# Hybrid transformer block: first stage unrolled into slots over a ring of three PSUM banks, exponentials scaled on GpSimd

## The reference

```python
x = x + _L0_attn_a_ref(_layernorm(x, axis=-1), L0_attn_a_Wq, ..., L0_attn_a_Wpost)
...
Q, K, V = X @ Wq, X @ Wk, X @ Wv          # 16 heads of 64
raw_attn = jnp.einsum('bshe,bthe->bsth', Q, K * inv_sqrt_d)
attn = jax.nn.softmax(raw_attn, axis=2)
A = jnp.einsum('bsth,bthe->bshe', attn, V)
A = jax.nn.gelu(A, approximate=False)
P = A @ Wpost
return X + P
```

## Time and profile before

| | |
|---|---|
| Median of 3 runs | 4349.55 us (4342.45 to 4356.19) |
| Profiled execution | 4354.61 us, span 4352.8 us, mean granted TensorE clock 0.963 |
| PE busy | 3920.6 us (90%) |
| DVE busy | 2631.3 us (60%) |
| ACT busy | 2414.3 us (55%) |
| POOL busy | 800.1 us (18%) |
| First stage | from the start to about 2449 us of the span |

### The profile page before, as it was taken

The page is one execution under the profiler, slowest core; times in us unless marked ns, Lnnn a source line. Parts: engine busy times, 40 slices in busy tenths (PEclk is TensorE's granted clock), DMA queues, the critical chain, the costliest instruction groups (busy, mean ns, idle before and its releaser), DMA issues. The chain is left out here.

```text
span 4352.8 us, 65779 instructions
## 1 busy us (share of the span) xinstructions
PE 3920.6 (90%) x24194; PEld 2770.9 (64%) x24194; DVE 2631.3 (60%) x3989; ACT 2414.3 (55%) x4705; POOL 800.1 (18%) x587
## 2 busy tenths in 40 slices
PE   6999999999999999999999568999999998999987
PEld 5777777777777777777777444555555555555544
DVE  5666666566656656665666446666666666666552
ACT  3565556556555655555565325555555555555554
POOL 0000000000000000000000143444444444343422
PEclk9999999999999999999999779999999999999998
DMA  4344334434333443443344222222222222222220
GB/s 120 81 106 97 83 88 97 98 78 107 88 85 85 92 99 84 100 97 83 79 106 93 62 49 45 50 50 50 50 50 50 50 50 50 49 49 48 45 43 15
DMA packets 152325, 315.67 MB, mean 73 GB/s; under 512 B 23072, under 2 KB 76704, under 8 KB 152032
## 3 DMA queue, kind: packets, MB, share of 16 engines
q1 hardware_dynamic: 152032, 311.39, 33.8%
HBM read 33.43 MB, written 25.17 MB: 13 GB/s over the span
## 5 line engine op out<-in xcount | busy, mean ns | idle before, releaser
L586 DVE TENSOR_REDUCE neg_max<-ps_s 128x2 f32<-128x1024 f32 x512 | 624.8, 1221 | 487.2 <-PE ps_s L361 487.2
L1168 DVE TENSOR_REDUCE max_b<-ps_s 128x2 f32<-128x1024 f32 x512 | 624.6, 1220 | 331.6 <-PE ps_s L952 330.4
L489 ACT ACTIVATE e_a<-ps_s,neg_max 128x512 f32<-128x512 f32 x1024 | 692.4, 685 | 87.8 <-DVE neg_max L586 82.1
L1051 ACT ACTIVATE et<-ps_s 128x1024 f32<-128x1024 f32 x512 | 522.4, 1020 | 353.7 <-PE ps_s L966 351.7
L525 ACT ACTIVATE et_a<-ps_t 128x512 f32<-128x512 f32 x512 | 306.6, 599 | 545.5 <-PE ps_t L242 545.4
L360 PE MATMUL ps_s<-stack_a 128*128 128x512 f32 x1024 | 445.1, 435 | 106.3 <-issue 72.4
L242 PE MATMUL ps_t<-ident,e_a 128*128 128x128 f32 x4096 | 531.5, 273 | 4.6 <-issue 2.6
L242 PEld LDWEIGHTS ps_t<-ident,e_a 128*128 128x128 f32 x4096 | 477.1, 140 | 78.3 <-ACT et_a L525 11.5
L376 PE MATMUL ps_o<-et_a,v_a 128*64 128x256 f32 x4096 | 498.3, 385 | 0.0
L910 POOL TENSOR_TENSOR h_lo<-h,h_hi 128x512 fp32r<-128x512 f32 x256 | 325.4, 1288 | 486.2 <-ACT h_hi L1087 484.1
L361 PE MATMUL ps_s<-stack_a 128*128 128x512 f32 x1024 | 414.6, 405 | 0.0
(11 more groups left out here) (189 smaller groups left out, 7186.2 us busy)
## 6 DMA issues: line engine op xcount, KB each, us to landing
stack_a<-raw_a SPq DMA_DIRECT2D x256, 384.0 KB, 4.7
stack_a<-raw_a SPq DMA_DIRECT2D x256, 256.0 KB, 4.3
stack_a<-raw_a SPq DMA_DIRECT2D x256, 128.0 KB, 4.0
q_stack<-roped_q SPq DMA_DIRECT2D x256, 64.0 KB
k_stack<-roped_k SPq DMA_DIRECT2D x256, 64.0 KB
x_next<-X SPq DMA_DIRECT2D x16, 512.0 KB, 6.7
X<-res SPq DMA_DIRECT2D x16, 512.0 KB, 2.9
x_ahead<-X SPq DMA_DIRECT2D x16, 512.0 KB, 3.9
```

The lines of the kernel that those rows point to most:

```text
L489: ins = nc.scalar.activation(e_a[u % 2][:, j, :], ps_s[:, 2 * (u % 2) + j, :], ACT.Exp, bias=neg_max[:, u % 4, j:j + 1], accum_out=sums[:, ...
L586: nc.vector.reduce_max(neg_max[:, u % 4, :], ps_s[:, 2 * (u % 2):2 * (u % 2) + 2, :], AX.X, negate=True)\
L1051: nc.scalar.activation(et[:, v % 5, :, :], ps_s[:, 2:4, :], ACT.Exp)\
L1168: nc.vector.reduce_max(max_b[:, u // 4 % 2, :, u % 4], ps_s[:, 0:2, :], AX.X, negate=True)\
```

## The change

All units of all sequences, 512 of them, become one row of *slots* without blocks, barriers or a hardware loop. In slot `s`, PE makes the scores of unit `s + 2`, the transposes of unit `s`, in every fourth slot the values of a whole pair (32 matmuls), and then what `todo_of` lists for the slot: a transpose of x, a q or k projection, two values projections, or a quarter of the output projection. The slots count from the start of a sequence: q and k of a pair are made in slots with remainder 1 and 2 when divided by 4, the values projections and the output projection in those with remainder 3, and `values` in those with remainder 0.

Every product that leaves through a bank, the two halves of the transposes among them, takes the next bank of a ring of three (`ps_t` 0, `ps_t` 1, `ps_m`) in the order of the program, and waits until the product three places earlier has been emptied. `e_a` has three buffers in place of two, `et_a` five in place of four, `parts` five in place of four.

The softmax division moves ahead of the transposes: DVE inverts the two sums of a unit, and GpSimd multiplies the unit's exponentials (128x1024) by them in one operation, whose second operand repeats one number 512 times. `recip_rows`, the copy to `rs_a`, the spreading copy and `norm` are gone. Gelu reads `ps_o` directly, pair by pair, and GpSimd makes the low half of its split. The row sums of the output projection no longer stay in four banks for all pairs: two groups of four pairs are added to `res` one after the other.

```diff
-        def attention_a(seq, before, now, ahead):
...
+                def normalise_exps(u):
+                    pool.wait_ge(recip_ready, u + 1)
+                    factor = recip[:, u % 4, :].rearrange("p (j o) -> p j o", o=1).to_broadcast([P, 2, S])
+                    nc.gpsimd.tensor_tensor(e_a[:, u % 3, :, :], e_a[:, u % 3, :, :], factor, ALU.mult).then_inc(e_normed, 1)
+
+                def heads_low(n):
+                    pool.wait_ge(heads_high, n + 1)
+                    nc.gpsimd.tensor_tensor(parts_of(n)[:, 1, :], heads_a[:, n % 2, :], parts_of(n)[:, 0, :], ALU.subtract)\
+                        .then_inc(parts_ready, 1)
...
+                def transposes(u):
+                    pe.wait_ge(e_normed, u + 1)
+                    for part in range(2):
+                        fill = fill_of["turn", part, u]
+                        if fill >= 3:
+                            wait_emptied(pe, fill - 3)
...
+                for slot in range(FIRST, LAST):
+                    if 0 <= slot + 2 < UNITS_ALL:
+                        scores(slot + 2)
+                    if 0 <= slot < UNITS_ALL:
+                        transposes(slot)
+                    if slot % 4 == 0 and 1 <= slot // 4 <= PAIRS * BATCH:
+                        values(slot // 4 - 1)
+                    for todo in todo_of.get(slot, []):
+                        product(todo)
...
+                def gelu(n):
+                    act.wait_ge(values_done, n + 1)
+                    if n >= 2:
+                        act.wait_ge(parts_ready, n - 1)
+                    nc.scalar.activation(heads_a[:, n % 2, :], ps_o[:, :], ACT.Gelu).then_inc(gelu_done, 1)
+
+                for slot in range(FIRST, LAST):
+                    for todo in todo_of.get(slot - 1, []):
+                        high(todo)
+                    if 0 <= slot < UNITS_ALL:
+                        copy_turned(slot)
+                    if (slot - 1) % 4 == 0 and 1 <= (slot - 1) // 4 <= PAIRS * BATCH:
+                        gelu((slot - 1) // 4 - 1)
+                    if 0 <= slot + 2 < UNITS_ALL:
+                        exps(slot + 2)
...
+                for slot in range(FIRST, LAST):
+                    if 0 <= slot + 1 < UNITS_ALL:
+                        invert(slot + 1)
+                    for todo in todo_of.get(slot - 1, []):
+                        low(todo)
+                    if 0 <= slot + 2 < UNITS_ALL:
+                        unit_max(slot + 2)
+                    if 0 <= slot < UNITS_ALL:
+                        copy_turned(slot)
```

More of the change, by code:

```diff
@@ L236, in token_major, with bank, wait_filled, wait_emptied @@
             return last
[L238 to L250, removed]
+        def bank(fill):
+            return banks[fill % 3]
+        def wait_filled(engine, fill):
+            engine.wait_ge(bank_filled[fill % 3], fill // 3 + 1)
+        def wait_emptied(engine, fill):
+            engine.wait_ge(bank_freed[fill % 3], fill // 3 + 1)
+        def emptied(ins, fill):
+            ins.then_inc(bank_freed[fill % 3], 1)
         with nc.Block() as block:
@@ new lines, in hybrid_block_kernel @@
+        UNITS_ALL = BATCH * UNITS
+        XT, QK_FIRST, VALUE_SLOTS = -9, -7, ((-5, -5, -1, -1), (11, 11, 15, 15))
+        POST = ((19, 23), (35, 39))
+        STATS, AGGREGATE, POWER, NORMALISE = (-19, -18), -17, -17, (-15, -14)
+        RESIDUAL, LOAD_X, SAVE_X, STACK_FIRST = 11, -20, 40, -5
+        FIRST, LAST = -20, UNITS_ALL + 9
+        todo_of = {}
+        for s in range(BATCH):
+            for k in range(KT):
+                todo_of.setdefault(UNITS * s + XT, []).append(("x", k, 0, s))
+            for p in range(PAIRS):
+                for i in range(2):
+                    todo_of.setdefault(UNITS * s + QK_FIRST + 4 * p + i, []).append(("qk", p, i, s))
+            for g in range(2):
+                for tok in range(TB):
+                    todo_of.setdefault(UNITS * s + VALUE_SLOTS[g][tok], []).append(("v", g, tok, s))
+            for half in range(2):
+                for two in range(2):
+                    todo_of.setdefault(UNITS * s + POST[half][two], []).append(("post", half, two, s))
@@ L404, in _ @@
-                    if now:
-                        scores(0)
-                        scores(1)
-                    if before:
-                        for k in range(PAIRS):
-                            if k >= 4:
-                                pe.wait_ge(heads_split, k - 3)
-                            for t in range(TB):
-                                for i, (part, w) in enumerate(((0, wpost_hi), (0, wpost_lo), (1, wpost_hi))):
-                                    last = mm(wide_banks[t][:, 0:D], heads_parts[:, k % 4, part, t * P:(t + 1) * P],
-                                              w[:, k, :], start=(k == 0 and i == 0), stop=(k == PAIRS - 1 and i == 2))
-                                if k == PAIRS - 1:
-                                    last.then_inc(post_done, 1)
-                            if k < PAIRS - 1:
-                                last.then_inc(parts_used, 1)
@@ L457, in _ @@
-                    if ahead and not now:
-                        for k in range(KT):
-                            transpose_x(k)
-                        for m in range(3):
-                            project_ahead(m)
-                    if now:
-                        values(2 * PAIRS - 1)
-                    if ahead:
-                        project_ahead(3)
-                    if now and not ahead:
-                        pe.wait_ge(rs_ready, PAIRS - 1)
-                        recip_rows(PAIRS - 1)
@@ L469, in _ @@
-                    if ahead:
-                        for g in range(2 * TB):
-                            if g >= 4:
-                                pe.wait_ge((va_even, va_odd)[g % 2], (g - 4) // 2 + 1)
-                            token_major(ps_s[:, g % 4, :], xh_a, xl_a, wa_hi, wa_lo, g // 2, 2 * DA + (g % 2) * S, S)\
-                                .then_inc(va_proj, 1)
-                            if g == 0 and now:
-                                pe.wait_ge(lo_ready, projs + 4)
-                                recip_rows(PAIRS - 1)
@@ L680, in attention_a, with product @@
-            next_block()
-        attention_a(-1, False, False, True)
-        attention_a(0, False, True, True)
-        with nc.Fori(1, BATCH - 1) as seq:
-            attention_a(seq, True, True, True)
-        attention_a(BATCH - 1, True, True, False)
-        attention_a(BATCH, True, False, False)
+                                          et_a[:, (4 * n + 2 * half + h) % 5, t, :], start=(t == 0), stop=(t == TB - 1))
+                    last.then_inc(values_done, 1)
+                def product(todo):
+                    kind, a, b, s = todo
+                    fill = fill_of[todo]
+                    if fill >= 3:
+                        wait_emptied(pe, fill - 3)
+                    if kind == "x":
+                        pe.wait_ge(xn_ready, TB * (s + 1))
+                        for t in range(TB):
+                            last = nc.tensor.transpose(bank(fill)[:, t * P:(t + 1) * P], xn_a[:, t, a * P:(a + 1) * P], ident[:, :])
+                    elif kind == "qk":
+                        if a == 0 and b == 0:
+                            for k in range(KT):
+                                wait_emptied(pe, fill_of["x", k, 0, s])
+                        last = feature_major(bank(fill), xh_a, xl_a, wa_hi, wa_lo, b * DA + a * P)
+                    elif kind == "v":
+                        last = token_major(bank(fill), xh_a, xl_a, wa_hi, wa_lo, b, 2 * DA + a * S, S)
+                    else:
+                        pe.wait_ge(parts_ready, PAIRS * s + 4 * a + 4)
+                        for t in (2 * b, 2 * b + 1):
+                            for k in range(4):
+                                p = 4 * a + k
+                                parts = parts_of(PAIRS * s + p)
+                                for m, (part, w) in enumerate(((0, wpost_hi), (0, wpost_lo), (1, wpost_hi))):
+                                    last = mm(bank(fill)[:, (t % 2) * D:(t % 2 + 1) * D], parts[:, part, t * P:(t + 1) * P],
+                                              w[:, p, :], start=(k == 0 and m == 0), stop=(k == 3 and m == 2))
+                    last.then_inc(bank_filled[fill % 3], 1)
@@ L690, in hybrid_block_kernel @@
+        next_block()
         with nc.Block() as block:
```

528 lines of the change are left out of this document (235 added, 293 removed).

## The result

The changed kernel takes 4786.6 us (median of 4 runs, 4775.5 to 4793.7) against 4352.9 us (median of 4 runs) for the kernel before: 1.0996 times the time before, 95% interval 1.0963 to 1.1028. The profiled execution took 4787.6 us, with a span of 4785.8 us and a mean granted clock of 0.919 (before 0.963).

The account below looks back on a forecast made before the run. TensorE's own stream was taken to bound the first stage. Waits of 576 us less a gain of 310 gave +266, the clock +109: +375 on 4354.6, 4730, as median 4725 us; range 4470 to 4880.

Parts of the forecast that it names:

- the walk: Step-by-step timing of one pair through TensorE, ScalarE and VectorE in the changed order: 20.9 us, where it was 18.8.
- TensorE's own work: TensorE's matmuls for a pair in the changed order, summed from distances of starts, without waits: 16.4 us.
- gross gain: First stage: time saved if TensorE never waited, 16 sequences x 19.4 us = 310 us.
- First wait: TensorE waits before the second projection for the first projection's bank, behind Gelu and table loads: 3.75 us per pair.
- Second wait: TensorE's next product waits for the second projection's bank to be emptied: 0.75 us per pair.
- the clock: TensorE's granted clock falls after the recurring wait: 0.85 us per pair, +109 us in all.
- Half of the bound: Clock price per pair lies between 0 and 1.7 us; half of it, 0.85, was taken.
- Rival 1: The clock holds in most pairs of the first stage, so only the waits cost: 4616 us; chance 0.27.
- GpSimd: Its product with the repeated operand takes 2.40 us per unit, costs nothing, and decides only beyond 3.4 us.
- Rival 2: GpSimd becomes the bound if the repeated operand makes its product twice as dear, 4.8 us: 4950 us; chance 0.09.
- Rival 3: ScalarE's chain is shorter: 4290 us if loads cost no time, 4040 if never last; chance 0.09 together.
- Rivals 4 and 5: 4: about 2 us of chain hidden, clock holds, effects cancel, chance 0.04; 5: smaller loss, up to 4560, chance 0.08.

Follow-up runs that it names:

- e8: Changed kernel with Exp pair ahead of Gelu, both projections' high parts early, and VectorE's reciprocal behind the copy in remainder-3 slots: 4199.7 us, 0.9653 of the kernel before.
- e9: e8 with Copy in place of Gelu, so without table loads: 4174.5 us, 0.9589 of the kernel before.
- e1: Changed kernel with ScalarE's Copy in place of Gelu, so no table loads in the first stage: 4307.9 us, 0.9895 of the kernel before.
- e10: e3 with a tiny Exp right behind Gelu, so the load for Exp comes at once: 4774.2 us, 1.0968 of the kernel before.
- e2: Changed kernel with 13 idle matmuls per pair filling TensorE's wait before the second projection: 4668.6 us, 1.0718 of the kernel before.
- e6: Changed kernel with GpSimd's product made twice for each unit, first into a spare tile: 4813.6 us, 1.1058 of the kernel before.
- e7: e8 with GpSimd's product made twice for each unit: 4520.9 us, 1.0384 of the kernel before.
- e3: Changed kernel with the Exp pair moved ahead of Gelu and its loads in slots with remainder 1: 4565.3 us, 1.0481 of the kernel before.
- e4: e3 with the first projection's high part also moved ahead of Gelu and the loads: 4574.4 us, 1.0508 of the kernel before.

## Why the prediction was right

Forecast 4725 us in 4470 to 4880, slower with 0.87; measured 4787. The mechanism was the one of the walk: the loads in ScalarE's order hold the first projection's bank, TensorE waits for it once a pair, and the clock falls behind the wait. All times below are per pair and from start to start.

- **TensorE's own work**, 16.4 us: undersized by 0.3. Where nothing is late, the traces of the changed kernel, e8 and e9 give 3 x 0.92 + 1.04 for the scores, 3 x 0.79 + 0.97 for the transposes, 2 x 1.48 for the projections, 3.60 for the values, 2.88 as the mean of two values projections (2.80) and a quarter of the output projection (2.96), and 0.10 for the transposes of x, which the sum lacked: 16.7. So the gross gain would be 128 x (18.8 - 16.7) = 269 us, not 310; e8, which still has 0.7 us of short waits, gets 179 of it in the first stage's period.
- **First wait**, 3.75 us: right. The transposes in front of the second projection take 1004.23 - 999.80 = 4.43 us where 0.79 would do, so it starts 3.64 us late. The profile calls 3.4 of this idle time, since the transposes' results come 0.24 us after their last issue. e1 (0.6 of 3.4 left without loads) and e10 (back to 3.5 with one load) show the chain.
- **Second wait**, 0.75 us, and **the clock**, 0.85: they exclude each other, and the forecast added them. In the 16 pairs in which the clock held, the third product starts 0.6 us late. In the others slower matmuls fill that time. Over all pairs the second projection takes 2.43 us in place of 1.48, the scores behind it 1.41 in place of 0.92, the transposes 1.13 in place of 0.79: 1.8 us together, against a forecast of 1.6. e2 shows what of this comes back with the clock held, 0.9. Half of the bound was a choice between 0 and 1.7 and not worked out; that it came near was luck.
- **Rival 1** is out: the clock fell in 103 of 119 pairs, and its mean is 0.91 between the first and last sequence.
- **GpSimd**, 2.40 us, costed at nothing: it takes 1.89, and e6 shows that even 3.8 costs 27 us in all. The 2.9 above it came from a row that the earlier trace rows do not show (1286 ns, `q_rot`, in the same trace), and L923's 1568 ns, 3.1 a column, is not close to 2.4; neither changed the term. Rival 2 is out here, though its reasoning is right: e7, with the bound away, loses 321 us to it.
- **Rival 3**, a chain without the loads' time: e1 is that kernel, forecast at 4290, measured 4308. It did not happen since each load is a row of 1283 ns in ScalarE's order, with nothing that hides it. Rivals 4 and 5 asked for a hidden part of the chain or a loss up to 4560; neither is there.

Put together for a pair: 16.7 of own work + 3.6 of first wait + 1.8 of clock and second wait = 22.1, as measured. The forecast was 16.4 + 3.75 + 1.6 = 21.75. e2 nearly adds up too: 16.7 + 3.7 for the first wait, filled, and what is left of it + 0.9 for the second and a short one = 21.3, where 21.2 were measured.

As to the rule on table sets: by the 2.66 us per switch of the Trainium skill (ScalarE: Activation LUTs, "What ACT_TABLE_LOAD costs") I had estimated some 350 us more. No run shows the second part of that price: in e10 the load starts 0.01 us after Gelu's end, in e3 0.02 us after the Exp pair's last row. A switch costs 1.4 us here: its load of 1283 ns, and the 0.1 us by which the operations on its two sides would have overlapped (1.91 us from start to start in the changed kernel, 0.50 without a load in e3). The measurement decides. But the rule itself, in the Trainium skill, ScalarE: Activation LUTs, "Table sets", to group one set's work, names the cost that decided here, and e1 puts it at 479 us in the wrong place.

## What to carry to other kernels

When a long operation is put into an engine's stream, follow who waits for the operations queued behind it: 2.6 us of table loads per pair, on an engine busy 55% of the time, made the pair 3.8 us longer (22.1 against 18.4 in e1), because a bank's release stood behind them. A ring of banks makes every late emptier a wait for the third product after it, whatever that product is; so order each engine's slot by what others wait for, releases first, long things with slack last: here nearly the same instructions in another order took 587 us less. Once a wait recurs in every round, reckon with a second price from the clock (118 us net here), but do not add to it a later wait that the slower work would fill. And read small waits from the starts: a busy share of 99% still held 0.7 us of them in 17.4.

## What the runs showed of the hardware

- A product on GpSimd whose second operand repeats one number per row takes 1.89 us for 128x1024, in place or into another tile (e7), against 2.40 us for the sum of two full tensors. Product or sum is not the reason: on 128x512 full tensors a product takes 1.30 us and a difference 1.29 (e7, L845 and L836).
- ScalarE's copies ran under the table of Gelu as well as under that of Exp: the load for Exp stands at the next Exp (e3), so copies can be put between Gelu and that load.
- A switch between the two tables costs 1.4 us in a stream without gaps: 1283 ns for the load and 0.1 us of lost overlap.
- A recurring wait of 3.4 us in 22 us brings the mean granted clock of the stage to 0.91, one of 2.0 us in 20.5 (e3) to 0.92, one of 2.2 us in 20.5 (e4) to 0.95; with one of 0.6 us in 18.4 (e1) it is 1.00. Idle matmuls in the wait of 3.4 us bring the clock back to 1.00 and gain 118 us, though they add 1625 instructions.
